# Row maxima of an attention stage: one in eight taken through a Relu of key differences on ScalarE, units of one bank, and TensorE's work per key tile in another order

## What is computed

```
qkv = (x @ Wqkv).reshape(b, l, 3, H, DH)
q, k, v = (qkv[:, :, 0], qkv[:, :, 1], qkv[:, :, 2])
...
q = q * cos + rotate_half(q) * sin
k = k * cos + rotate_half(k) * sin
scale = DH ** (-0.5)
scores = jnp.einsum('bqhd,bkhd->bhqk', q, k) * scale
attn = jax.nn.softmax(scores, axis=-1)
out = jnp.einsum('bhqk,bkhd->bqhd', attn, v)
```

## Time and profile before

| what | value |
|---|---|
| median of 3 runs | 2123.95 us |
| lowest and highest | 2120.16 and 2124.56 us |
| the profiled execution's own time | 2122.61 us |
| its span | 2120.8 us |
| TensorE busy, share of the span | 95% |
| VectorE busy | 87% |
| ScalarE busy | 72% |
| 30 full iterations, 862.80 to 1967.90 us | 1105.10 us, 36.84 us each |

### The profile page before, as it was taken

One profiled execution on the slowest core, in us unless ns is written; L12 is line 12 of the kernel. 1 busy time (PEld: TensorE's weight loads), 2 busy tenths in 40 slices (PEclk: granted clock), 3 DMA queues, 4 the chain that ended last, 5 costly groups with the idle time before them and its releaser, 6 DMA issues. The chain is left out here.

```text
span 2120.8 us, 46870 instructions
## 1 busy us (share of the span) xinstructions
PE 2011.0 (95%) x18498; PEld 798.8 (38%) x18498; DVE 1838.1 (87%) x2195; ACT 1523.0 (72%) x3579; POOL 764.6 (36%) x1019
## 2 busy tenths in 40 slices
PE   7889999999998886999999999999999999999978
PEld 5444455555553432333333333333333333333333
DVE  3697888898886775999999999999999999999255
ACT  0155676666663413999999999999999999999911
POOL 2499899999998203603003003002000000052100
PEclk9999999999999757999999999999999999999989
DMA  8365565566567414302002001001000000031321
GB/s 279 125 140 124 127 153 136 143 158 157 127 149 161 114 34 102 81 7 55 5 7 54 7 15 46 4 25 36 5 27 5 7 24 7 9 121 58 98 71 53
DMA packets 228811, 161.86 MB, mean 76 GB/s; under 512 B 152809, under 2 KB 199865, under 8 KB 228585
## 3 DMA queue, kind: packets, MB, share of 16 engines
q1 hardware_dynamic: 198272, 112.61, 21.5%
q0 software_dynamic: 14944, 31.33, 5.5%
q10 hardware_dynamic: 15376, 14.93, 2.1%
HBM read 97.64 MB, written 44.11 MB: 67 GB/s over the span
## 5 line engine op out<-in xcount | busy, mean ns | idle before, releaser
L1422 ACT ACTIVATE pr<-ps_s 128x512 f32<-128x512 f32 x2048 | 1087.1, 596 | 72.7 <-PE ps_s L1335 25.9
L1433 DVE TENSOR_REDUCE mx<-ps_m 128x2 f32<-128x1024 f32 x980 | 1124.3, 1213 | 10.6 <-PE ps_m L1311 8.9
L1353 PE MATMUL ps_o<-pr,vg 128*32 128x256 f32 x8192 | 654.8, 392 | 8.1 <-ACT f_ou L1413 8.1
L588 POOL TENSOR_TENSOR room<-qs 128x512 f32<-128x512 f32 x336 | 414.8, 1268 | 79.7 <-ACT qs L855 54.4
L1335 PE MATMUL ps_s<-qs,ks 50*128 50x512 f16 x2048 | 423.2, 382 | 0.5 <-ACT pr L1422 0.5
L1311 PE MATMUL ps_m<-ks,qs 48*128 48x512 f16 x1960 | 384.5, 388 | 9.4 <-PEq L322 9.4
L1267 POOL DMA_DIRECT2D vg<-vb_d x24 | 19.6, 819 | 976.3 <-PE ps_o L1353 893.9
L1353 PEld LDWEIGHTS ps_o<-pr,vg 128*32 128x32 f32 x8192 | 162.6, 108 | 273.6 <-issue 245.6
L1311 PEld LDWEIGHTS ps_m<-ks,qs 48*128 48x128 f16 x1960 | 93.9, 92 | 413.0 <-issue 278.1
L927 DVE TENSOR_TENSOR room<-PSa,qs 128x512 f32<-128x512 f32 x368 | 234.1, 678 | 14.1 <-PE PSa L681 13.6
L1335 PEld LDWEIGHTS ps_s<-qs,ks 50*128 50x128 f16 x2048 | 188.8, 94 | 119.9 <-ACT pr L1422 38.6
(11 more groups left out here) (162 smaller groups left out, 1906.9 us busy)
## 6 DMA issues: line engine op xcount, KB each, us to landing
room<-skew SPq DMA_DIRECT2D x128, 208.0 KB, 4.0
skew<-attn SPq DMA_DIRECT2D x64, 164.0 KB, 4.2
tail_room<-in_W SPq DMA_DIRECT2D x32, 256.0 KB, 3.4
tail_room<-in_W2T SPq DMA_DIRECT2D x32, 256.0 KB, 4.1
vb_d<-vb SPq DMA_DIRECT2D x8, 1024.0 KB, 6.0
qs<-ks SPq DMA_DIRECT2D x26, 256.0 KB, 5.7
ks<-k_d POOLq DMA_DIRECT2D x48, 128.0 KB, 3.2
qs<-q_d POOLq DMA_DIRECT2D x180, 32.0 KB, 2.9
```

What stands on the lines that cost most here:

```text
L588: pool.tensor_tensor(prod_p[:, n % RING, :], qT[:, c, :], kT[:, c, col:col + CH], ALU.mult).then_inc(prod_p_ready, 1)
L1353: mm = pe.matmul(ps_o[SLOT * j:SLOT * (j + 1), cols], vg[:, kt, j, :], pr[:, kt % PR_RING, j, cols], start=(kt == 0 and part == 0), stop=( ...
L1422: act.activation(pr[:, kt % PR_RING, j, :], ps_s[:, place_of(y, n) % SB, :], ACT.Exp, scale=exp_scale).then_inc(p_ready, 1)
L1433: dve.tensor_reduce(mx[:, x % MX_RING, :, pair * TILES + tile, quarter], ps_m[:, u % 2, :, :], AX_X, ALU.max).then_inc(m_read, 1)
```

## The change

1. **Units of one bank.** A unit of maxima is now one head of a pair (t alternates), so one matmul and one reduction of 512 values; 64 units per iteration, 4 per tile. Three banks hold them; the scores have four (SB = 4).
2. **Eight units are a cycle** (two tiles), with the key quarters in the order 0, 2, 1, 3. Unit 1 of a cycle ("less") is the product of the queries with the *difference* of the keys of quarter 0 and quarter 1 (`kd`). ScalarE takes its Relu into `over`. Unit 5 ("both") is the plain product with quarter 1; VectorE adds `over` to it and takes the maximum of the sum in one `tensor_tensor_reduce` (max(a, b) = b + relu(a - b)). The assembler makes two instructions of it: the operation, and one that writes out the accumulator. So of eight units VectorE reduces six, joins one, and leaves one to ScalarE.
3. **TensorE's order in a tile** is new: maximum, weigh part 0, then maximum and score in turns, with a maximum ahead of each of the first two scores. Part 0 of `weigh` takes 320 queries and part 1 takes 192.
4. **Key differences** are made in the local stage for heads t = 1: the rotated keys of the first chunk of a sequence are kept in `first_k`; in the next chunk (j = 1 and j = 5) VectorE subtracts, ScalarE rounds, VectorE makes the remainder, ScalarE sends it out; the dense stage loads it into `kd` (three DMAs more per group).
5. `mx` is set to the lowest f32 number where the "less" units no longer write.

```diff
-    (68.079, "last", 3)]
+    (68.079, "last", 3), (68.9, "diff", 2), (69, "diff", 3), (76.8, "diff_last", 2), (77.2, "diff_last", 3)]
...
-    (66.977, "rest", 2), (71.781, "rest", 3)]
+    (66.977, "rest", 2), (71.781, "rest", 3), (71.9, "diff", 2), (72, "diff", 3), (74.8, "diff_rest", 2), (75, "diff_rest", 3)]
...
+                elif what == "diff" and j % NCH == 1:
+                    act.wait_ge(diff_ready, j // NCH * 2 + i - 1)
+                    act.copy(first_parts[:, i % 2, 0, :], rope_q[:, i % 2, :]).then_inc(diff_high, 1)
...
+                elif what == "diff" and j % NCH == 1:
+                    dve.wait_ge(qparts_ready, j * 4 + i + 1)
+                    dve.tensor_tensor(rope_q[:, i % 2, :], first_k[:, i % 2, :], rope_q[:, i % 2, :],
+                                      ALU.subtract).then_inc(diff_ready, 1)
...
-    MAXU = MAXIMA * NCH
+    MAXU = 2 * MAXIMA * NCH
...
+    CYCLE, LESS, BOTH = 2 * NCH, 1, 5
+    QUARTERS = (0, 2, 1, 3)
+    START = FIRST + CYCLE
+    M_BANKS = 3
...
-    SB = 3
+    SB = 4
...
+    FIRST_QUERIES = 320
-    QK_LOADS = 16 * 6 * (1 + NCH)
+    QK_LOADS = 16 * (6 * (1 + NCH) + 3)
...
+            def max_unit(n, q, slot):
+
+                old = n - M_BANKS
+                if old >= FIRST:
+                    if is_less(old):
+                        pe.wait_ge(m_over, overs(old + 1))
+                    else:
+                        pe.wait_ge(m_read, reads(old + 1))
+                t, pair, tile, quarter = unit_place(n)
+                rows = half(t, 0, KROWS)
+                keys = kd[rows, slot, pair, :] if is_less(n) else ks[rows, slot, pair, quarter * CH:(quarter + 1) * CH]
+                pe.matmul(ps_m[:, n % M_BANKS, :], qs[rows, q, pair, tile * P:(tile + 1) * P], keys,
+                          start=True, stop=True).then_inc(m_ps, 1)
...
-                cols = slice(CH // 2 * part, CH // 2 * (part + 1))
+                cols = slice(FIRST_QUERIES, CH) if part else slice(0, FIRST_QUERIES)
...
+                    if x == 1 and kt == (START - FIRST) // PER_TILE:
+                        pe.wait_ge(kd_ld, 16 * len(K_STACK))
+                    older = y * KT + kt - LAG
                     tile_max(x, PER_TILE * kt)
+                    if older >= 0:
+                        weigh(older // KT, older % KT, 0)
+                    tile_max(x, PER_TILE * kt + 1)
                     score(x, GRP * kt, q, slot)
+                    tile_max(x, PER_TILE * kt + 2)
                     score(x, GRP * kt + 1, q, slot)
...
-                    older = y * KT + kt - LAG
                     if older >= 0:
-                        weigh(older // KT, older % KT, 0)
-                    tile_max(x, PER_TILE * kt + 1)
+                        weigh(older // KT, older % KT, 1)
+                    tile_max(x, PER_TILE * kt + 3)
                     score(x, GRP * kt + 2, q, slot)
                     score(x, GRP * kt + 3, q, slot)
-                    if older >= 0:
-                        weigh(older // KT, older % KT, 1)
...
+            def take_less(n):
+                k = overs(n)
+                if k >= 2:
+                    dve_unit = n - 2 * CYCLE + BOTH - LESS
+                    act.wait_ge(m_read, reads(dve_unit + 1))
+                act.wait_ge(m_ps, n - FIRST + 1)
+                act.activation(over[:, k % 2, :], ps_m[:, n % M_BANKS, :], ACT.Relu).then_inc(m_over, 1)
...
+                        unit = (y + 1) * MAXU + CARRY + n + 1
+                        if is_less(unit) and unit < ITERS * MAXU:
+                            take_less(unit)
                         act.wait_ge(s_ps, y * SCORES + n + 1)
...
+                if is_both(n):
+                    dve.wait_ge(m_over, overs(n))
+                    above = over[:, (overs(n) - 1) % 2, :]
+                    dve.tensor_tensor_reduce(out=above, in0=ps_m[:, n % M_BANKS, :], in1=above, scale=1.0, scalar=LOWEST,
+                                             op0=ALU.add, op1=ALU.max, accum_out=best).then_inc(m_read, 1)
+                else:
+                    dve.tensor_reduce(best, ps_m[:, n % M_BANKS, :], AX_X, ALU.max).then_inc(m_read, 1)
```

More of the change, by code:

```diff
@@ L434, in parts, with rotated @@
             return (qparts_last if j == NG - 1 and i >= 2 else qparts)[:, i % 2]
+        def rotated(j, i):
+            return (first_k if j % NCH == 0 and i >= 2 else rope_q)[:, i % 2, :]
         def qk_banks(j, i):
@@ L896, in step @@
                     act.wait_ge(rope_sum, j * 4 + i + 1)
-                    act.copy(parts(j, i)[:, 0, :], rope_q[:, i % 2, :]).then_inc(rope_high, 1)
+                    act.copy(parts(j, i)[:, 0, :], rotated(j, i)).then_inc(rope_high, 1)
+                elif what == "diff" and j % NCH == 1:
+                    act.wait_ge(diff_ready, j // NCH * 2 + i - 1)
+                    act.copy(first_parts[:, i % 2, 0, :], rope_q[:, i % 2, :]).then_inc(diff_high, 1)
+                elif what == "diff_last" and j % NCH == 1:
+                    act.wait_ge(diff_parts, j // NCH * 2 + i - 1)
+                    dst = D["kd_d"][:, (i % 2) * (HD // 2):(i % 2 + 1) * (HD // 2), :, j // NCH * CH:(j // NCH + 1) * CH]
+                    act.dma_start(dst.rearrange("s d h t -> (d h) s t"), first_parts[:, i % 2]).then_inc(diff_stored, 16)
                 elif what == "last":
@@ L1219, in _ @@
         def _(sp):
+            load_differences(sp, 0, kd_ld)
             for n in range(2, NCH):
@@ L1447, in max_rows @@
                 dve.tensor_copy(nmt[:, :], ps_s[0:PARTS * 16, bank, 0:P // 2].bitcast(F16)).then_inc(nmt_sb, 1)
+            plain = (START - MAXU) // CYCLE
+            for ring, first in ((0, 0), (1, plain), (2, 0)):
+                lower(ring, first, MAXIMA)
             for x in range(1, ITERS):
                 for e in range(MAXU):
-                    u = CARRY + e
-                    if x + u // MAXU < ITERS:
-                        max_unit(x + u // MAXU, u % MAXU)
-                    if 0 <= u - MAXU < NM_STEPS:
-                        max_parts(x, u - MAXU)
+                    n = x * MAXU + CARRY + e
+                    if n < ITERS * MAXU and not is_less(n):
+                        max_unit(n)
+                    part = (CARRY + e - MAXU) // 2
+                    if CARRY + e >= MAXU and e % 2 == 0 and part < NM_STEPS:
+                        max_parts(x, part)
+                        if x == 1 and part == NM_STEPS - 1:
+                            lower(1, 0, plain)
                     if e == PER_TILE * ROWS_KT:
```

63 lines of the change are left out of this document (47 added, 16 removed).

## The result

The changed kernel takes **2153.16 us** (median of 4 runs, 2148.17 to 2161.93), the kernel before 2122.05 in the same comparison. The ratio is **1.0143, 95% interval 1.0109 to 1.0176**: 1.4% slower. The forecast was 2141, with 2110 to 2167 as its range. The profiled execution lasted 2155.57 us, its span is 2153.5.

The account below looks back on a forecast made before the run. VectorE was taken to bound the kernel before. Dense iterations +16, the end -1 and the local stage +2 gave +17, so 2122.6 became 2139.6, and 1.34 for the median made 2141 us; range 2110 to 2167.

Parts of the forecast that it names:

- Direction and mechanism of the dense stage: Dense attention's 30 iterations: TensorE becomes slowest, 37.37 us per iteration against 36.84 before, +16 us; slower case 0.64.
- the wait: `weigh` in each dense iteration: waits 1.3 us (1.1 to 1.45) for ScalarE's copy of the output, 0.26 before.
- the parts: TensorE's two `weigh` parts per dense tile: 0.68 us for part 0, 0.46 for part 1, from 0.57 each.
- The joined operation: VectorE's add and maximum in the dense stage: 0.69 us with accumulator read-out, between 0.60 and 0.80.
- the much slower rival: VectorE's joined operation in the dense stage runs at half rate, 1.22 us: +72 us, about 2196; chance 0.06.
- Slips of the banks: Maxima's three banks in the dense stage: units start late, 0.3 us per iteration, bounds 0 and 0.9.
- The transposes: TensorE's transposes of the maxima in each dense iteration: 0.27 us more, 0.58 where 0.31 was.
- The step that failed: Operations added to the local stage for key differences: mostly hidden behind TensorE and GpSimd, 0 to 6 us, taken as 2.
- The even rival: Dense iterations: bank slips cost nothing, copy wait at its lower bound, 36.9 us each, 2124 to 2128; chance 0.20.
- The faster rival: Dense iterations: the output's copy gets through in time, wait stays 0.26 us, -20 us, 2105; chance 0.10.
- The end: Last iteration and the six tiles before it: ScalarE's slots shrink from 0.505 to 0.49 us, -1 us.

Follow-up runs that it names:

- e1: The changed kernel with ScalarE's output copy two exponentials earlier (OUTPUT_AT 4 instead of 6): 2119.72 us, ratio 1.0008 to the kernel before.
- e2: The changed kernel with ScalarE's output copy one exponential earlier (OUTPUT_AT 5 instead of 6): 2142.31 us, ratio 1.0126 to the kernel before.
- e4: The kernel before with the changed kernel's local stage, key differences stored but not used: 2135.60 us, ratio 1.0092 to the kernel before.
- e9: The changed kernel's dense stage with the local stage of before, first chunk's keys loaded instead of differences: 2145.55 us, ratio 1.011 to the kernel before.
- e3: The changed kernel with VectorE's `diff_rest` and ScalarE's `diff_last` later in the local stage's order: 2140.12 us, ratio 1.0115 to the kernel before.
- e5: e3 with the output copy two exponentials earlier (OUTPUT_AT 4): 2115.92 us, ratio 0.9983 to the kernel before.
- e11: e5 with two equal parts of `weigh`, 256 queries each instead of 320 and 192: 2111.98 us, ratio 0.9949 to the kernel before.
- e8: The changed kernel with ScalarE's output copy three exponentials earlier (OUTPUT_AT 3 instead of 6): 2132.30 us, ratio 1.0052 to the kernel before.

## Why the prediction was right, and where it was not

**Direction and mechanism of the dense stage: right.** TensorE became the bound, and paid for the copy. The forecast put +16 us into the 30 iterations, and +16.6 came. Step by step: the copy 4.4 us after the first score (measured 4.34), the waiting `weigh` 5.1 after it (5.16), the wait 1.3 (1.33 here, 40.0 / 30), a tile 2.2 us (1229.35 - 1227.13 = 2.22), the parts 0.68 and 0.46 (`weigh` at 1227.67 to the maximum at 1228.13 is 0.46), an iteration 37.37 (37.39). e1 and e2 show that the wait is paid in full, at 0.49 us per place in ScalarE's queue.

**The joined operation: right.** I took 0.69 with its read-out. The two rows of it:

```profile
L1513 DVE CUSTOM_DVE_ANT_0 over<-ps_m,over x244: 683/692/693, 861.3 to 1997.3; 128x512 f32<-128x512 f32 x122
L1513 DVE DVE_READ_ACCUMULATOR2_ANT mx<- x244: 82/83/85, 862.0 to 1997.9; 128x1 f32 x122
```

The operation lasts 0.69, the read-out 0.08, and from 1229.77 to the next reduction at 1230.39 it is 0.62. The Trainium skill (Vector Engine (DVE) Microarchitecture Reference, "Points that are easy to get wrong") names a halved throughput for this family with two sources in SBUF that are not bf16. With one source in PSUM it does not strike here (0.69 us), and the much slower rival falls.

**Two terms inside the iteration were off and cancelled.** Slips of the banks were put at 0.3: TensorE's tiles keep 2.22 us but for 0.02 to 0.03 in three of them, so they cost below 0.1. The transposes were put at 0.27 more: tile 12 takes 2.65 instead of 2.22, 0.43 more. And tile 1, which has the wait, takes 1.40 more than 2.22, where 1.3 was booked. (Medians of the 30 iterations.)

**The step that failed is the local stage**, "0 to 6, I take 2". e4 measures 13 to 26 us for it alone, and 12.8 in its profiled execution. I had seen one in-order wait, ScalarE at `diff` for VectorE; the dear one goes the other way, VectorE at `diff_rest` for ScalarE, with L260 and thus TensorE behind it (6.16 us there, 12 in all around it). I had set the rows of a mean load (VectorE 70 of 80 us) against it, which says nothing of an instruction at the head of an in-order queue. A third part was not in the sum at all: where TensorE stands that long, its granted clock falls to 0.50 behind it, 3.8 us in the changed kernel. The other part is size: I took 0.68 for each added operation, but the two subtractions, whose operands all lie in SBUF, took 1.63 each (3.26 for two). The row at which this could have been seen is in the trace of before, an operation of the same kind that lasts 0.67 to 1.81:

```profile
L1059 DVE TENSOR_TENSOR qparts<-tail_room,qparts x30: 673/688/1814, 248.3 to 820.0; 128x512 f16<-128x512 f32 x30
```

**That the time still lies in the range is in part luck.** Its upper end, 2167, had 26 us above the forecast, nearly all for bank slips and a longer wait in the dense stage. Those didn't come, and the local stage's miss used their room: 12.8 to 17 us where its own bound was 6.

**The even rival** needed an iteration of 36.9: it did not come. **The faster rival** had its point of decision right, "if the copy starts less than 3.6 us after the first score": e1 moves the copy there (3.38 us, median), and the loss in the dense stage turns into a gain of 0.42 us per iteration. It got there by two places in the queue, not by itself.

**The end** was put at -1; the changed kernel's profile has -2.7, e9's +0.7. These are single executions and I read nothing from them.

*What stays open.* How much of the 7 us in e3, e5 and e11 would go if the subtractions took their usual 0.68: the waits behind them are in the traces, but no run took GpSimd, beside which they are slow (below), away. And the spread of whole times: the changed kernel's runs lie 14 us apart, those of the kernel before up to 18 in one group, while iterations repeat to 0.01 us; which part of the rest of the program varies was not looked into.

## What to carry to other kernels

When an engine hands a buffer over through another engine's queue, count the operations that stand ahead of the hand-over in that queue; moving the consumer earlier, or putting one operation more ahead of the producer, is paid in full once the consumer is at its own floor, and here two places (1.0 us per iteration) were the difference between 1.4% slower and even. Try the first place at which the data is ready, and not one before it: in e8 the engine that waited there pushed back all that followed. And a step inserted in an order table is priced at its worst in-order wait, in both directions, with the work that stands behind it, not by the mean load of the engine.

## What the runs showed that I had not expected

- ScalarE's slots shrink when it has a backlog: exponentials start every 0.494 us in the kernel before and every 0.477 in the changed one (median), while their mean duration grows from 596 to 632 ns. The duration of one is no measure of the rate.
- VectorE's two-input f32 operations of 512 values with both operands in SBUF: 1.63 us each at 367 us, 0.67 for the one at 388.07, the same engine and nearly the same operation within 21 us. GpSimd tells them apart. In the changed kernel's trace 34 of the 104 such operations had GpSimd busy for less than 30% of their time, and none of them took over 0.693 us; 24 lay beside GpSimd's own products L597 (running for over 90% of their time) and took 1.59 in the median. The 265 with an operand in PSUM that lay beside L597 took 0.627 to 0.693. The other 12 traces look the same (0.695 at most where GpSimd is idle, medians of 1.53 to 1.59 beside L597). It is a correlation, since no run took GpSimd away.
- Single-bank reductions cost what two-input operations cost: 0.60 from start to start for either, so joining a sum to a maximum is free but for the read-out of the accumulator.
